# A new beginning and a new end of attention in a gated cross-attention and MLP block

## The reference

```
def ln(x): return (x - mean(x)) / sqrt(var(x) + 1e-5)          # over the last axis
q, k, v = ln(x), ctx, ctx            # each (16, 8 heads, 16, 256)
qk  = einsum('bhdq,bhdl->bhql', q, k) / 4
att = gamma * einsum('bhql,bhdl->bhdq', softmax(qk), v)
x   = x + tanh(g_xattn) * att
def qmm(x, w, s): return (x @ float8_e4m3(w)) * s               # weights rounded to e4m3
h   = ln(x)
y   = qmm(silu(qmm(h, gate_w, gate_scale)) * qmm(h, up_w, up_scale), down_w, down_scale)
out = x + tanh(g_ffn) * y            # hidden size 256, inner size 768
```

## Time and profile before

| | us |
|---|---|
| median of 3 runs | 214.7 (214.63 to 214.72) |
| profiled execution, its own time | 213.49 |
| its span, first to last instruction | 211.7 |
| PE busy | 198.6 |
| DVE busy | 159.3 |
| POOL busy | 145.7 |
| ACT busy | 125.0 |
| mean granted TensorE clock | 0.974 of full |

### The profile page before, as it was taken

One profiled execution on the slowest core, in us unless ns is written; L12 is line 12 of the kernel. 1 busy time (PEld: TensorE's weight loads), 2 busy tenths in 40 slices (PEclk: granted clock), 3 DMA queues, 4 the chain that ended last, 5 costly groups with the idle time before them and its releaser, 6 DMA issues.

```text
span 211.7 us, 4722 instructions
## 1 busy us (share of the span) xinstructions
PE 198.6 (94%) x1785; PEld 120.9 (57%) x1785; DVE 159.3 (75%) x336; ACT 125.0 (59%) x242; POOL 145.7 (69%) x167
## 2 busy tenths in 40 slices
PE   8569999999999999999999998999799999999991
PEld 5236456665665566556654553446566666766581
DVE  3799899999999997698968617055957676765985
ACT  2012758776877586768776774369547544854450
POOL 5994779957999999983799302384554899567440
PEclk9975899999999999999999999999999999999999
DMA  6799601101122231232311412311320003003033
GB/s 177 228 351 388 125 2 53 31 26 49 53 91 70 65 127 31 59 117 67 101 58 50 121 39 55 102 51 51 113 90 10 2 3 99 0 0 99 5 99 99
DMA packets 19783, 17.75 MB, mean 84 GB/s; under 512 B 4016, under 2 KB 19248, under 8 KB 19760
## 3 DMA queue, kind: packets, MB, share of 16 engines
q1 hardware_dynamic: 19760, 17.44, 26.6%
HBM read 11.02 MB, written 6.42 MB: 82 GB/s over the span
## 4 chain that ended last, share of the span: by engine, by line
PE 79%; DVE 12%; ACT 3%; issue 2%; POOL 1%; DMA 1%; SPq 0%; DVEq 0%; ACTq 0%; POOLq 0%
PE ps L727 19%; PE ps L791 17%; PE ps L768 13%; PE ps L739 12%; PE ps L852 9%; DVE neg_max L545 6%; PE ps L742 4%; PE ps L755 2%; PE ps L752 2%; ACT p_t L468 1%; DMA c_sb<-in_ctx 1%; PE ps L778 1%; ACT xn L497 1%; DVE p_t L701 1%; DVE p_t L696 1%
## 5 line engine op out<-in xcount | busy, mean ns | idle before, releaser
L545 DVE TENSOR_REDUCE neg_max<-ps 128x2 f32<-128x512 f32 x128 | 79.5, 683 | 11.8 <-PE ps L727 11.6
L468 ACT ACTIVATE p_t<-ps 128x512 f32<-128x512 f32 x128 | 66.9, 600 | 20.9 <-PE ps L742 18.9
L727 PE MATMUL ps<-km,qn 32*128 32x512 f32 x256 | 74.6, 651 | 3.7 <-POOL qn L351 3.2
L739 PE MATMUL ps<-qm,c_sb 32*128 32x512 f32 x256 | 74.6, 651 | 1.3 <-ACT p_t L468 1.3
L791 PE MATMUL ps<-w_exp,w_gu 128*128 128x512 f16 x192 | 45.2, 380 | 1.3 <-DVE w_exp L596 1.2
L434 POOL TENSOR_TENSOR f_lo<-fu,f_hi 128x512 fp32r<-128x512 f32 x23 | 29.3, 1279 | 21.5 <-ACT f_hi L486 21.5
L742 PE MATMUL ps<-max_t,sel 4*128 4x256 bf16 x256 | 35.1, 274 | 0.0
L742 PEld LDWEIGHTS ps<-max_t,sel 4*128 4x128 bf16 x256 | 18.8, 96 | 23.1 <-issue 20.7
L768 PE MATMUL ps<-p_t,v_t 128*32 128x256 f32 x512 | 30.9, 382 | 0.4 <-ACT p_t L468 0.4
L662 DVE SCALAR_TENSOR_TENSOR ga<-th,ps 128x512 f32<-128x512 f32 x24 | 16.4, 682 | 19.6 <-ACT th L481 19.6
L739 PEld LDWEIGHTS ps<-qm,c_sb 32*128 32x128 f32 x256 | 27.3, 188 | 5.8 <-issue 2.9
(11 more groups left out here) (69 smaller groups left out, 228.1 us busy)
## 6 DMA issues: line engine op xcount, KB each, us to landing
u_scr<-u_sb SPq DMA_DIRECT2D x32, 128.0 KB
u_n<-u_scr SPq DMA_DIRECT2D x16, 128.0 KB
r_n<-r_scr SPq DMA_DIRECT2D x16, 128.0 KB
out_x<-p_t SPq DMA_DIRECT2D x16, 128.0 KB, 1.9
x_sb<-in_x SPq DMA_DIRECT2D x3, 512.0 KB, 8.9
c_sb<-in_ctx SPq DMA_DIRECT2D x3, 512.0 KB, 8.9
w_all<-in_L_ffn_gate_w SPq DMA_DIRECT2D x1, 768.0 KB, 9.2
w_all<-in_L_ffn_up_w SPq DMA_DIRECT2D x1, 768.0 KB, 9.8
```

The lines of the kernel that those rows point to most:

```text
L468: nc.scalar.activation(p_t[:, b % 2, i, :], ps[:, bank_of["t", n][0], :], ACT.Exp, scale=DH ** -0.5).then_inc(exp_ok, 1)
L545: nc.vector.tensor_reduce(neg_max[:, b % 2, at:at + PAR, 0], ps[:, bank_of["s", n][0], :].rearrange("p (e l) -> p e l", e=PAR), axis=AX.X, ...
L727: nc.tensor.matmul(ps[:, bank, :], qn[rows, b % 2, P * t:P * (t + 1)], km[rows, b % 2].rearrange("p e l -> p (e l)"), start=True, stop=Tru ...
L739: nc.tensor.matmul(ps[:, bank, :], c_sb[rows, b, P * t:P * (t + 1)], qm[rows, b % 4].rearrange("p e l -> p (e l)"), start=True, stop=False)
```

## The change

Beginning: DVE makes batch 0's masked keys; means are negated once (`neg_m`) and queries are made with add in place of subtract, in `norm_apply_first` too; masked queries are a function of their own (`masked`) and stand later at the start; statistics are taken in smaller portions (`STATS`); weight blocks are spread over later batches; there are 20 dummy matmuls instead of 25.

End of attention: one ring of all 8 banks to the last fill. The first chunk's transposes ("X") come one and a half batches earlier, before P(12). The last two batches follow `LAST_STEPS`, in which gate steps 0, 1 and 2 ("G") stand between groups of "t" fills and between the last two P. Two copies of P results (batches 13 and 14) move from ACT to DVE (`u_copy`). ACT's and DVE's orders there are rewritten to match, and POOL makes two low parts before `attention(2)`. In the MLP, `norm_chunk(2)`, `norm_chunk(3)`, `rstd_chunk(2)`, `rstd_chunk(3)`, `attention(3)` and the last reciprocals move by one to two steps.

```diff
+LAST_STEPS = "tttPTttttGttttGtttttQGR"
+EARLY = 3
+STATS = {0: (4, 6), 1: (6, 8), 4: (8, 11), 5: (11, 14), 7: (14, 15), 9: (15, 16)}
-HALF_BINADES = (1, 2, 4, 5, 6, 8)
-HALF_ROUNDED = (2, 3, 5, 6, 7, 8)
+HALF_BINADES = (2, 3, 6, 8, 9, 10)
+HALF_ROUNDED = (3, 4, 6, 8, 10, 11)
 # bank_table
-    for b in range(NB):
+    for b in range(NB - 2):
         for kind in STEP:
+            if kind == "P" and b == NB - 3:
+                order += [("X", 0), ("X", 1)]
...
+    order.append(("s", FILLS * NB - 1))
+    for kind in LAST_STEPS:
...
-        if at > last_plain:
-            bank = 2 + at % (RING - 2)
-        if kind == "t" and n >= total - FILLS:
-            bank = 3 + n % 3
-        if kind == "P" and n >= NB - 2:
-            bank = 7
 # POOL
+                if n > 0:
+                    nc.gpsimd.tensor_scalar(neg_m[:, lo:hi], mv[:, lo:hi, 0], -1.0, None, ALU.mult).then_inc(nm1_ok, 1)
...
-                nc.gpsimd.tensor_scalar(qn[:, b % 2, :], x_sb[:, b, :], mv[:, b, 0:1], rstd[:, b:b + 1],
-                                        ALU.subtract, ALU.mult).then_inc(qn_ok, 1)
+                nc.gpsimd.tensor_scalar(qn[:, b % 2, :], x_sb[:, b, :], neg_m[:, b:b + 1], rstd[:, b:b + 1],
+                                        ALU.add, ALU.mult).then_inc(qn_ok, 1)
...
-            keys(0)
             pow_group(0)
             queries(0)
             keys(1)
             pow_group(1)
             queries(1)
             nc.gpsimd.memset(nm_parts[:], 0.0).then_inc(consts, 1)
+            masked(0)
...
+            low(0, 0)
+            low(1, 1)
             attention(2)
...
-                    if c == 0 and it == 4:
+                    if c == 1 and it == 0:
                         rstd_chunk(2)
-                    if c == 1 and it == 2:
+                    if c == 1 and it == 3:
                         attention(3)
-                    if c == 2 and it == 0:
+                    if c == 2 and it == 1:
                         rstd_chunk(3)
 # ACT, in place of the last two batches of the loop
+            for i in range(3):
+                exps(NB - 2, i)
+            max_out(NB - 1)
+            v_out(NB - 1)
+            for i in range(3, 7):
+                exps(NB - 2, i)
+            act.wait_ge(coef_ok, 2)
+            gate_tanh(0, 0)
+            exps(NB - 2, 7)
+            for i in range(3):
+                exps(NB - 1, i)
+            gate_tanh(1, 1)
+            fused_high(0, 0)
+            for i in range(3, FILLS):
+                exps(NB - 1, i)
+            fused_high(1, 1)
+            norm_apply(1)
+            gate_tanh(2, 2)
+            act.wait_ge(u_ok, NB - 1)
+            u_save(NB - 1)
 # DVE
+            stats_batches(0, 1)
+            v.wait_ge(ag1_ok, 1)
+            nc.vector.tensor_scalar(neg_m[:, 0:1], mv[:, 0, 0:1], -1.0, None, ALU.mult).then_inc(nm0_ok, 1)
+            v.wait_ge(c_in[0], 16)
+            for e in range(PAR):
+                nc.vector.tensor_scalar(km[:, 0, e, :], c_sb[:, 0, :], mask[:, e:e + 1], None, ALU.mult).then_inc(k0_ok, 1)
...
-            stats_group(0)
-            stats_group(1)
+            stats_batches(1, 4)
...
+                if b == 14:
+                    v.wait_ge(t_ok, 1)
+                    nc.vector.tensor_copy(x_t[:, 0, 0], ps[:, PS_T0:PS_T0 + HT, :]).then_inc(hi_ok, 1)
+                    chunk_low(0, PS_T0)
...
+            u_copy(NB - 3)
             v.wait_ge(coef_ok, 3)
+            products(0, 0)
+            products(1, 1)
+            u_copy(NB - 2)
+            products(2, 2)
...
-                    if c == 0 and it == 4:
-                        reciprocals(3)
+                    if (c, it) == (0, 5):
+                        reciprocals(3)
-                    if (c, it) in ((0, 3), (1, 5)):
-                        norm_chunk(c + 2)
+                    if (c, it) in ((0, 5), (2, 0)):
+                        norm_chunk(3 if c else 2)
 # TensorE
-            for _ in range(25):
+            for _ in range(20):
...
+            n = FILLS * (NB - 2)
+            scores(FILLS * NB - 1)
+            for i in range(3):
+                scores_t(n + i)
+            weighted(NB - 3)
+            turn(NB - 1)
+            for i in range(3, 7):
+                scores_t(n + i)
+            gate_up(0, 0)
+            for i in range(7, 11):
+                scores_t(n + i)
+            gate_up(0, 1)
+            for i in range(11, 2 * FILLS):
+                scores_t(n + i)
+            weighted(NB - 2)
+            gate_up(0, 2)
             weighted(NB - 1)
```

More of the change, by code:

```diff
@@ L410, in _ @@
                     queries(b + 2)
+                    masked(b + 2)
                 if b in HALF_ROUNDED:
@@ L501, in _ @@
             v_out(0)
-            for b in range(NB):
+            for b in range(NB - 2):
                 for i in range(FILLS):
                     exps(b, i)
-                    if i == 4 and b + 1 < NB:
+                    if i == 4:
                         max_out(b + 1)
@@ L714, in bank_free @@
                     pe.wait_ge(u_ok, held[1] + 1)
+                if held is not None and held[0] == "X":
+                    pe.wait_ge(lo_ok, 1)
+                if held is not None and held[0] == "G":
+                    pe.wait_ge(fu_ok, held[1][0] + 1)
             def scores(n):
@@ L775, in transposes @@
                 pe.wait_ge(n2_ok, CH * (c + 1))
+                if c == 1:
+                    for ht in range(HT):
+                        bank_free(last_use[bank + ht])
                 for q in range(CH):
@@ L785, in gate_up @@
                     pe.wait_ge(lo_ok, c + 1)
-                if n >= 2:
+                if n == 0:
+                    pe.wait_ge(w_ok, 6)
+                for m in range(2):
+                    if n < EARLY:
+                        bank_free(bank_of["G", (n, m)][1])
+                    elif n < EARLY + 2:
+                        bank_free(last_use[gate_bank(n, m)])
+                if n >= EARLY + 2:
                     pe.wait_ge(fu_ok, n - 1)
@@ L813, in _ @@
                 scores_t(n + 3)
-                if b == NB - 1:
-                    pe.wait_ge(w_ok, 6)
-                    for half in range(2):
-                        bank_free(last_use[gate_bank(0, half)])
-                    gate_up(0, 0)
                 scores_t(n + 4)
@@ L821, in _ @@
                 scores(m + 4)
+                if b == NB - 3:
+                    for ht in range(HT):
+                        bank_free(bank_of["X", ht][1])
+                    transposes(0, PS_T0)
                 if b > 0:
                     weighted(b - 1)
-                if b + 1 < NB:
-                    turn(b + 1)
+                turn(b + 1)
                 scores(m + 5)
@@ L831, in _ @@
                 scores_t(n + 7)
-                if b == NB - 2:
-                    pe.wait_ge(max_ok, FILLS * NB)
-                    for bank in range(PS_T0, PS_T0 + HT):
-                        bank_free(last_use[bank])
-                    transposes(0, PS_T0)
-                if b == NB - 1:
-                    gate_up(0, 1)
+            n = FILLS * (NB - 2)
[14 more added lines that the diff above has]
+            gate_up(0, 2)
             weighted(NB - 1)
@@ L848, in down @@
                         pe.wait_ge(yo_ok, c)
+                    else:
+                        for half in range(2):
+                            bank_free(last_use[PS_Y + half])
                 for q in tiles:
```

105 lines of the change are left out of this document (64 added, 41 removed).

## The result

| | us |
|---|---|
| before, median of 4 runs | 214.66 (214.28 to 214.72) |
| after, median of 4 runs | 220.09 (219.41 to 220.51) |
| after / before | 1.0254 (95%: 1.0224 to 1.0284) |
| profiled execution after: time, span | 220.3, 218.5 |

The account below looks back on a forecast made before the run. TensorE's work plus its holes was taken to bound the kernel; 2.1 + 1.4 + 5.7 - 2.0 = 7.2 off the 211.7 span gave 204.5, a median of 207.5 us. Range 205.4 to 209, with rivals 1 to 3 to 211.2.

Parts of the forecast that it names:

- The middle: Regular batches up to P(12): spread weight blocks and statistics and an earlier last `qn` give 7.07 us each, gain 1.4.
- the rule: DVE and POOL operations hold a shared SBUF port pair exclusively, the second waits whole; keys push POOL's power by up to 0.7.
- the spread of 560 to 791 ns: DVE's weight operation, one shape at unequal prices beside a busy POOL; taken to agree with the port rule in direction.
- the two new keys: Start: DVE makes batch 0's masked keys, 2 x about 0.34 us, taking 0.96 of POOL's keys off the chain.
- Rival 1: POOL's add costs what its subtract does: middle -0.5 instead of 1.4, start 0.2 less, 209.6 us; chance 0.22.
- The clock rival: Start: fewer dummies and holes keep TensorE's clock low longer; at 20 us longer 215.7 us; chance 0.07.
- `qn` at add: POOL's queries with add instead of subtract: 0.5 us taken, 1.24 kept in the range.
- The start: Up to the second turn: earlier first maximum and less DVE stall, gain 2.1 us, bounds 1.0 and 4.1.
- The end of attention: X to chunk 1's first gate laid out by hand at 32.4 us, 6.1 less; gain 5.7, bounds 3 and 6.5.
- the 0.4 given back for joints: End of attention: 0.4 us taken off the 6.1 for two tight waits and joints of different shapes, leaving 5.7.
- Chunk 3: MLP: POOL's later rstd and norm of chunk 3 delay ACT and a gate step; loss 2.0 us, bounds 0 and 3.

Follow-up runs that it names:

- e1: Changed kernel, with POOL's rounding and attention(0) made to wait for DVE's exponents of the same batch: 205.88 us, ratio 0.9644 to the kernel before.
- e4: Changed kernel with only `qn` made with subtract again, the slow form: 209.45 us, ratio 0.9796 to the kernel before.
- e5: Kernel before with one edit, means negated and `qn` made with add: 223.46 to 231.22 us, ratio 1.0449 from the first two runs.
- e12: Changed kernel, no gate, DVE's work between batches issued after the second maximum instead of the fourth: 208.62 us, ratio 0.9759 to the kernel before.
- e9: e1 with `rstd_chunk(3)` alone moved one step earlier: 205.68 us, ratio 0.961 to the kernel before.
- e11: e9 with 20 and 8 dummy matmuls put into TensorE's two waits of the start: 204.55 us, ratio 0.9584 to the kernel before.
- e6: Changed kernel with beginning and middle of the kernel before; new end of attention and MLP moves stay: 211.02 us, ratio 0.9868 to the kernel before.
- e3: Changed kernel with the weight blocks in the batches of the kernel before: 217.11 us, ratio 1.0146 to the kernel before.
- e10: e5 with POOL's rounding, but not attention(0), gated on DVE's exponents as in e1: 219.55 to 224.9 us over four runs, no ratio.

## Why the prediction was wrong

- **The step that failed is "The middle"**: "Regular batches then are 7.07 throughout ... Gain 1.4." It was a loss of 11.46 up to P(11). I summed POOL's work and DVE's work each for itself, with durations from a trace in which DVE happened to start first, and took POOL's earlier arrival as slack. e1, e4, e5 and e12 show what stands in its place: DVE's tensor-scalar operations wait behind POOL's rounding and attention, 11.8 us of added DVE time in four batches.
- The prediction had the rule in hand. It read the spread of 560 to 791 ns as the price of meeting POOL, 0.2, and asked only about the two new keys. Those 0.2 were the price when DVE is first, or meets one of POOL's short or slow-form operations. With a long POOL operation first the price is what is left of it: two exponents against two roundings, 3.1 in place of 0.2 a block. Rival 1 was built on a `qn` that stays slow; in truth the fast one was the danger, and no rival had it. The clock rival (215.7, chance 0.07) had the right sign and a wrong place: the start's low stretch cost 1.4, and the two in the middle, 2.8 together, came behind holes that DVE had opened.
- `qn` at add: 0.5 taken, 0.553 measured. Right, and it is what did the harm.
- The start: 2.1 forecast, 0.65 came. The two keys on DVE took 0.63, and the first maximum came at 6.62 (6.8 forecast). The mechanism was right; the low-clock stretch began 1.76 earlier and ended 1.65 later. 3.41 longer at 0.41 is 1.4, the difference. Where the low stretch was shorter, the gain is there: P(0) came 2.3 earlier than before in e9's profile (6.83 us low) and 2.6 in e11's (none).
- The end of attention: 32.4 laid out, 32.18 measured; -6.3 forecast for the whole row, -6.28 measured. The order holds, and e6 shows it alone; that the row agrees to 0.02 is luck, since X came 0.7 late and the 0.4 given back for joints and 0.2 of the layout were not needed.
- Chunk 3: 2.0 forecast, 2.27 measured; POOL's `shift` was the waited-for, as the step had it. ACT waited 3.39 for it (before 1.07).
- With the middle's waits taken away (e1), the span is 206.5 against the forecast 204.5: 1.7 of the 2.0 is the start, 0.3 chunk 3.

## What to carry to other kernels

Before making an operation on POOL faster or moving it, lay both engines' SBUF operations on one time line, and see which comes first at each meeting: if DVE is the engine that TensorE waits for and comes second, it can pay all that is left of POOL's operation (1.6 of 1.81 at 36.56). A wait on the engine with slack, or issuing the critical engine's operation earlier, makes the order certain; a tuned order that holds by 0.1 us is luck. Unequal durations of one shape are the sign to look for in the profile, before the change.

## What was not expected of the hardware

- On POOL, (x - m) * r with two pointers took 1.24 us on 128x256 (f32), and (x + m) * r 0.55.
- An operation's length in the trace includes its wait for the other engine: six elements per partition took 0.15 to 2.32 us, so busy time is not work.
- A DVE reciprocal and the batch statistics were not held up beside POOL's rounding, nor were DVE's tensor-scalars beside POOL's slow `qn` or its power (the lines above).
- A hole's length did not tell whether the clock fell. In the change 3.4 us at the half clock followed holes of 1.56 and 3.12 us on TensorE, and none followed 1.27; before, none followed 1.25. But in e3 and e5 one hole of 1.56 and one of 1.55 were not followed by it, and in e10 a hole of 1.16 was and one of 2.12 was not. At the start the low stretch was 3.41, 6.83, 10.24 or 13.65 us in the profiles of these kernels (0 in e11), and moved the time by more than the smaller edits did.
